# Normalised features of the next layer made inside three stages, and the scan's selection matrix made one stage earlier

## What is computed

```python
h = h + _L0_attn_ref(_layernorm(h, axis=-1), ...)   # state-space scan, 16 states
h = h + _L0_ffn_ref(_layernorm(h, axis=-1), ...)    # 15 experts, and a shared expert
h = h + _L1_attn_ref(_layernorm(h, axis=-1), ...)   # gated recurrence (GRU)
h = h + _L1_ffn_ref(_layernorm(h, axis=-1), ...)    # ternary weights, gelu, layernorm
h = h + _L2_attn_ref(_layernorm(h, axis=-1), ...)   # linear attention

def _layernorm(x, axis=-1, eps=1e-05):
    m = jnp.mean(x, axis=axis, keepdims=True)
    v = jnp.var(x, axis=axis, keepdims=True)
    return (x - m) / jnp.sqrt(v + eps)
```

## Time and profile before

| | us |
|---|---|
| median of 3 runs (1618.41 to 1622.33) | 1618.63 |
| the profiled execution | 1631.85 |
| its span | 1630.1 |
| busy PE, DVE, ACT, POOL | 1137.5, 1096.1, 676.5, 477.9 |
| granted TensorE clock, mean, as a share of full speed | 0.774 |

### The profile page before, as it was taken

The page is one execution under the profiler, slowest core; times in us unless marked ns, Lnnn a source line. Parts: engine busy times, 40 slices in busy tenths (PEclk is TensorE's granted clock), DMA queues, the critical chain, the costliest instruction groups (busy, mean ns, idle before and its releaser), DMA issues. The chain is left out here.

```text
span 1630.1 us, 31525 instructions
## 1 busy us (share of the span) xinstructions
PE 1137.5 (70%) x9868; PEld 814.8 (50%) x9868; DVE 1096.1 (67%) x2322; ACT 676.5 (42%) x1332; POOL 477.9 (29%) x614
## 2 busy tenths in 40 slices
PE   4514887774479998684857868365588886469992
PEld 2211232223368885352545745144476774469882
DVE  3864999994936554547867754888677766446553
ACT  4514655552045553214425722243365664224440
POOL 0042677762355554520001100000033332231203
PEclk9557899995589998787877977588566555569996
DMA  6500000001043334212000000000022221101113
GB/s 203 190 3 10 1 1 0 1 1 46 1 140 90 118 90 132 72 39 78 1 1 1 1 1 0 0 0 0 28 79 77 89 92 53 46 24 44 44 31 110
DMA packets 33968, 78.92 MB, mean 48 GB/s; under 512 B 6839, under 2 KB 22899, under 8 KB 30963
## 3 DMA queue, kind: packets, MB, share of 16 engines
q1 hardware_dynamic: 26800, 57.51, 10.3%
q0 software_dynamic: 6912, 18.88, 4.2%
q10 hardware_dynamic: 144, 1.05, 0.2%
HBM read 61.38 MB, written 16.04 MB: 47 GB/s over the span
## 5 line engine op out<-in xcount | busy, mean ns | idle before, releaser
L942 POOL TENSOR_TENSOR scan_ch<-scan_hs,scan_ct 128x452 f32<-128x452 f32 x128 | 143.3, 1140 | 58.8 <-DVE scan_hs L1054 52.4
L967 PE MATMUL scan_py<-scan_ch,ident 128*128 128x452 f32 x256 | 131.9, 606 | 40.4 <-POOL scan_ch L942 30.8
L1054 DVE TENSOR_TENSOR_SCAN scan_hs<-scan_abar,scan_bx 128x452 f32<-128x452 f32 x128 | 134.0, 1096 | 0.6 <-ACT scan_abar L1016 0.5
L2558 POOL TENSOR_TENSOR mha_prob_lo<-mha_prob,mha_prob_hi 113x452 f16<-113x452 f32 x64 | 65.4, 1043 | 137.7 <-ACT mha_prob_hi L2719 137.7
L457 PE MATMUL m0x_ph<-m0x_xb,m_w_hi 128*128 128x128 f16 x456 | 99.2, 220 | 0.2
L458 PE MATMUL m0x_ph<-m0x_xb,m_w_hi 128*128 128x128 f16 x456 | 99.1, 219 | 0.0
L459 PE MATMUL m0x_ph<-m0x_xb,m_w_lo 128*128 128x128 f16 x456 | 98.7, 218 | 0.0
L967 PEld LDWEIGHTS scan_py<-scan_ch,ident 128*128 128x128 f32 x256 | 41.4, 195 | 111.1 <-POOL scan_ch L942 99.9
L1641 DVE TENSOR_SCALAR m3x_a<-m3x_ph,m3x_b 128x128 f32<-128x128 f32 x184 | 49.7, 345 | 68.9 <-ACT m3x_ah L1602 67.0
L1016 ACT ACTIVATE scan_abar<-ssm_dt,ssm_a 128x448 f32<-128x448 f32 x128 | 80.6, 638 | 23.2 <-DVE scan_hs L1054 21.8
L1638 DVE SCALAR_TENSOR_TENSOR m0x_a<-m0x_ph,m0x_b,m0x_gate 128x128 f32<-128x128 f32 x114 | 34.7, 347 | 75.8 <-issue 38.2
(11 more groups left out here) (699 smaller groups left out, 4033.0 us busy)
## 6 DMA issues: line engine op xcount, KB each, us to landing
mha_wbuf<-m3w SPq DMA_DIRECT2D x16, 1024.0 KB, 4.6
tok_wbuf<-m0w SPq DMA_DIRECT2D x15, 768.0 KB
m_out<-m0x_yo SPq DMA_DIRECT2D x57, 128.0 KB
m_out<-m3x_yo SPq DMA_DIRECT2D x23, 128.0 KB
m_rows<-m0f_parts SPq DMA_DIRECT2D x4, 448.0 KB
m_rows<-m3f_parts SPq DMA_DIRECT2D x4, 448.0 KB
out<-h SPq DMA_DIRECT2D x4, 448.0 KB
tok_pt_f<-patches SPq DMA_DIRECT2D x1, 1728.0 KB, 8.1
```

What stands on the lines that cost most here:

```text
L942: pool.tensor_tensor(ch[r][:], hs[r][:], ct[n % 2][:], ALU.mult).then_inc(weighed, 1)
L967: pe.matmul(py[c][:, 0:GT], core.ident[:], ch[u % R][:], start=n == 0, stop=n == NS - 1).then_inc(summed, 1)
L1054: dve.tensor_tensor_scan(hs[u % R][:], abar[c][:, 0:GT], bx[u % R][:], 0.0, ALU.mult, ALU.add).then_inc(scanned, 1)
L2558: pool.tensor_tensor(prob_lo[g][:], prob[g % 2][:], prob_hi[g][:], ALU.subtract).then_inc(p_low, 1)
```

## The change

**Selection matrix.** `ssm.sel` lives beside the other inputs of the scan. POOL makes it in `stage_ssm_inputs`: a memset and two selects on 128 x 32 numbers, then one copy that spreads each over 128 columns. In the scan it is only read.

**Features of the next layer.** A new class `NextFeatures` does the work of the two stages group by group inside shared (for gru), gru (for bgm) and bgm (for la). The six stages between them go. DVE takes statistics and moments of a group (`stats`, `moments`), POOL raises the variance to -0.5 and multiplies (`scale`), ACT normalises (`normalise`, into one of two buffers), PE transposes one half of the features (`turn`), ACT and DVE write the high and the low half (`high`, `low`). PSUM banks for this are taken from the stages: shared has two px and pg in place of three and gives two banks, bgm one `po` in place of two and gives one, gru gives one that was free.

```diff
+class NextFeatures:
+    def stats(self, dve, b):
+        dve.bn_stats(self.six[:, b, :], self.core.h[:, b, :]).then_inc(self.counted, 1)
+    def moments(self, dve, q):
+        g = slice(q * GB, (q + 1) * GB)
...
+        dve.wait_ge(self.counted, (q + 1) * GB)
...
+        dve.tensor_scalar(var, var, 1.0 / D, EPS, ALU.mult, ALU.add).then_inc(self.var_ready, 1)
+    def scale(self, pool, q):
...
+        pool.wait_ge(self.var_ready, q + 1)
+        pool.tensor_tensor(self.rstd[:, g], self.var[:, g], self.half[:, g], ALU.pow).then_inc(self.raised, 1)
+        pool.wait_ge(self.raised, q + 1)
+        pool.tensor_tensor(self.shift[:, g], self.nmean[:, g], self.rstd[:, g], ALU.mult).then_inc(self.rstd_ready, 1)
+    def normalise(self, act, q):
+        act.wait_ge(self.rstd_ready, q + 1)
+        need(act, self.turned, (q - 1) * KC)
+        for j in range(GB):
+            b = q * GB + j
+            act.activation(self.xr[q % 2][:, j, :], self.core.h[:, b, :], ACT.Identity, bias=self.shift[:, b:b + 1],
+                           scale=self.rstd[:, b:b + 1]).then_inc(self.normed, 1)
+    def turn(self, pe, q, c):
+        n = q * KC + c
+        pe.wait_ge(self.normed, (q + 1) * GB)
+        need(pe, self.lo_done, n + 1 - self.banks)
...
+    def high(self, act, q, c):
+        act.wait_ge(self.turned, n + 1)
...
+    def low(self, dve, q, c):
+        dve.wait_ge(self.hi_done, n + 1)
...
 # stage_ssm_inputs, POOL
+                made.step(pool.memset(sel_rows[:], 0.0))
+                for part in range(2):
+                    made.step(pool.affine_select(out=sel_rows[:], in_=sel_rows[:], compare_op=ALU.not_equal, fill=1.0,
...
+                made.step(pool.tensor_copy(ssm.sel[:].rearrange("p a n m -> p (a n) m"),
+                                           sel_rows[:].unsqueeze(2).to_broadcast([128, 2 * NS, 128])))
 # stage_ssm_scan, POOL and PE
-                made.step(pool.memset(sel[:], 0.0))
-                for part in range(2):
-                    made.step(pool.affine_select(out=sel[:], in_=sel[:], compare_op=ALU.not_equal, fill=1.0,
...
-                pe.wait_ge(sel_made, 3)
 # stage_shared, POOL and PE
-                combine.gather(pool, core)
+                nx.begin(pool)
+                combine.gather(pool, core, range(3 * GB))
+                nx.scale(pool, 0)
+                combine.gather(pool, core, range(3 * GB, NB))
+                for q in range(1, NG):
+                    nx.scale(pool, q)
...
+                    if q >= 2:
+                        for c in range(KC):
+                            nx.turn(pe, q - 2, c)
                     outputs(q - 1)
-                outputs(NG - 1)
+                outputs(NG - 1, (0, 1))
+                for c in range(KC):
+                    nx.turn(pe, NG - 2, c)
+                outputs(NG - 1, (2, 3))
+                for c in range(KC):
+                    nx.turn(pe, NG - 1, c)
 # stage_gru, ACT
                     round_state(n - 1)
+                    q, e = unit(n)
+                    if q >= 2 and e == 0:
+                        nx.normalise(act, q - 2)
+                    if q >= 2 and e == 2:
+                        nx.high(act, q - 2, 0)
+                    if q >= 3 and e == 0:
+                        nx.high(act, q - 3, 1)
 # stage_bit_gelu, DVE (PE: turn in slots 2 and 3; ACT: normalise in slot 1, high in 2 and 3)
+                def following(q, j):
+                    if j == 0:
+                        dve.wait_ge(o_free, (q + 1) * GB)
+                        for i in range(GB):
+                            nx.stats(dve, q * GB + i)
+                        nx.moments(dve, q)
+                    if j >= 2:
+                        nx.low(dve, q, j - 2)
-                for q in range(NG + 2):
+                for q in range(NG + 3):
...
+                        if q >= 3:
+                            following(q - 3, j)
 # program
-            stage_norm_stats(nc, core, tag + "s", core.h)
-            stage_features(nc, core, tag + "f", core.h)
-            stage()
+        stage_gru(nc, core, d, gru, lambda st: PrepareLate(st, d, glu, mha))
+        stage_bit_gelu(nc, core, d, gelu)
+        stage_linear_attention(nc, core, d, linear)
```

More of the change, by code:

```diff
@@ L25 @@
 EPS = 1e-5
+NS = 16
 def wait_alone(eng, core, sem, value):
@@ L1696, in __init__, with gather @@
         self.added, self.picks_added = st.sem("added"), st.sem("picks_added")
-    def gather(self, pool, core):
+    def gather(self, pool, core, batches=range(NB)):
         m = self.m
-        for b in range(NB):
+        for b in batches:
             j = b % GB
@@ L1837, in _ @@
                         middle.on_scalar(act, n)
+                        if q >= 2 and f == 2:
+                            nx.normalise(act, q - 2)
                     high(q, FC - 1)
+                    if q >= 2:
+                        for c in range(KC):
+                            nx.high(act, q - 2, c)
+                for q in (NG - 2, NG - 1):
+                    nx.normalise(act, q)
+                    for c in range(KC):
+                        nx.high(act, q, c)
             @block.vector
@@ L1847, in low, with add @@
                     combine.add(dve, core, q, f)
-                def add(q):
-                    for j in range(GB):
+                def add(q, tiles=range(GB)):
+                    for j in tiles:
                         p, b = j % 2, q * GB + j
@@ L1871, in _ @@
                     low(q, FC - 1)
+                    if q >= 2:
+                        for c in range(KC):
+                            nx.low(dve, q - 2, c)
                     if q:
                         add(q - 1)
-                add(NG - 1)
+                        measure(q - 1)
+                for j in range(GB):
+                    add(NG - 1, (j,))
+                    if j == 1:
+                        for c in range(KC):
+                            nx.low(dve, NG - 2, c)
+                measure(NG - 1)
+                for c in range(KC):
+                    nx.low(dve, NG - 1, c)
 def stage_gru(nc, core, d, w, late):
@@ L1908, in _ @@
                     pool.memset(drive[p][:, :, 0:1], 0.5).then_inc(edges, 1)
+                nx.begin(pool)
                 late.on_pool(pool)
+                for q in range(NG):
+                    nx.scale(pool, q)
             @block.tensor
@@ L2003, in add, with measure @@
                                                  ALU.mult, ALU.add).then_inc(o_free[p2], 1)
+                def measure(q):
+                    for j in range(GB):
+                        dve.wait_ge(o_free[j % 2], q * 2 + j // 2 + 1)
+                        nx.stats(dve, q * GB + j)
+                    nx.moments(dve, q)
                 for n in range(N):
@@ L2011, in _ @@
                         add(q - 2, (2, 3))
+                        measure(q - 2)
                     dve.wait_ge(sig_ready, n + 1)
@@ L2017, in _ @@
                         split(n - 1)
+                    if q >= 2 and e == 2:
+                        nx.low(dve, q - 2, 0)
+                    if q >= 3 and e == 0:
+                        nx.low(dve, q - 3, 1)
                     late.on_vector(dve, n)
                 split(N - 1)
+                nx.low(dve, NG - 3, 1)
                 add(NG - 2, (2, 3))
-                add(NG - 1, (0, 1, 2, 3))
+                measure(NG - 2)
+                add(NG - 1, (0, 1))
+                for c in range(KC):
+                    nx.low(dve, NG - 2, c)
+                add(NG - 1, (2, 3))
+                measure(NG - 1)
+                for c in range(KC):
+                    nx.low(dve, NG - 1, c)
 def stage_bit_gelu(nc, core, d, w):
```

149 lines of the change are left out of this document (107 added, 42 removed).

## The result

The changed kernel takes 1622.72 us (median of 20 runs), the kernel before 1616.46 (median of 20 on the same chip): ratio 1.0032, 95% interval 1.0018 to 1.0047. The medians differ by 6.3 us and the ratio stands for 5.2: slower, just over what can be told from no change. The two profiled executions are not typical: 1631.85 before, 1611.37 after, so their spans must not be subtracted; the places have to be compared one by one.

The account below looks back on a forecast made before the run. DVE was taken to set the pace in gru and bgm. The terms -11.2 - 24.8 + 18.4 + 9.9 + 9.3 + 3.3 gave +4.9 us on the 1618.63 median: 1624 us, range 1608 to 1636.

Parts of the forecast that it names:

- Scan start: Selection matrix made earlier, in ssmin, so DVE's first scan product comes sooner: a gain of 11.2 us, bounds 9 and 12.
- Borders: Last add to next stage's first product: 9.65 us (shared), 11.05 (gru, bgm); 31.8 in place of 56.6, gaining 24.8.
- M: DVE's measuring of one group of four tiles, 4 statistics and 7 moment operations in chain: 2.5 us.
- P: POOL's power and product on 4 columns per group, with hand-overs: 2.0 us, the power taken as 1.6.
- rival B: No change: POOL's power on four columns costs as on one, 6.8 us less, 1617; chance 0.22.
- N: ACT's normalising of one group, 4 scaled activations of 256 columns at 0.49 us each: 1.65 us.
- Rival C: Much slower: POOL's power is paid per column, 16.6 us more, 1640; chance 0.12.
- Delay 1: Stage tails: PE waits before its last tiles until group 2 is normalised; 6.8 shared, 6.3 gru, 5.3 bgm, sum 18.4 us.
- Delay 2: Inside the stages: added work on DVE and ACT's queue lengthens gru by 9.9 us, bgm by 9.3, shared by 3.3.
- At no cost: Shared's last twelve POOL gathers now stand behind scale(0), hidden by an existing wait of 8.02 us; removed Sqrt loads save nothing.
- A: Faster: added work in gru units 6 to 11 and bgm groups 3 and 4 is hidden in waits, 1606; chance 0.20.
- D: The scan does not start sooner because something else was as late: 11.2 us more, 1635; chance 0.06.

Follow-up runs that it names:

- Moving the tiles forward: Changed kernel with group 2's transposes behind the last two output tiles in the tails of shared and gru: 1607.95 us, ratio 0.995 to the kernel before.
- second profile of the changed kernel: The changed kernel measured and profiled once more, unaltered: 1625.32 us, ratio 0.9992 to the kernel before.
- The second batch: Runs sharing one chip: the changed kernel again, all features at the tails, two variants of gru's part; the kernel before had median 1630.5 us there.
- the doubled statistics: Kernel with the selection matrix and bgm's features inside gru, its eight statistics inside the units done twice: 1626.69 us, ratio 0.9977 to the kernel before.
- the kernel with the matrix alone: Kernel before with only the selection matrix made in ssmin: 1618.08 us, ratio 0.9922.
- the one with shared's part: Kernel before plus the selection matrix in ssmin and gru's features inside shared: 1615.97 us, ratio 0.9905.
- gru's part alone: Kernel before plus the selection matrix in ssmin and bgm's features inside gru: 1624.22 us, ratio 0.9964.
- bgm's part alone: Kernel before plus the selection matrix in ssmin and la's features inside bgm: 1625.81 us, ratio 0.9963.
- the tails with the moments on DVE and on POOL: Matrix in ssmin, all features at stage ends; last batch against before: DVE moments 1580.23 us (0.9763); POOL moments for groups 0 to 2 1593.91 us (0.9851).

## Why the prediction was right, and where it was not

The forecast was +4.9 us and 1624, from a median of three runs; with 20 runs it is +5.2 by the ratio (+6.3 between the medians) and 1622.7. By its own steps:

**Scan start**, -11.2: measured -11.3 (-11.0 counted from the same instruction before ssmin). The Trainium skill's warning (GPSIMD Engine Reference, section 8) that POOL contends with DVE instructions that read two inputs in SBUF is borne out by the trace: 1.96 us for 0.69, and ssmin's first product 1.0 us later, which is what I had put on that case. The gain did not come down to 10 even so: in the changed kernel's profile DVE reaches the scan 0.75 us later, counted from the same instruction, in the others between 0.1 sooner and 1.0 later.

**Borders**, 9.65, 11.05 and 11.05: measured 9.3, 10.9 and 12.5 (bgm's last measure stood behind a low half that waited for ACT until 937.45, while its last add had ended at 936.90).

**Prices.** M 2.5 was 2.55. P 2.0 was 1.4 (707.61 to 709.01): the power on four columns takes 1.02 us against 0.86 on one, so rival B's price was nearly the right one (1.25). N 1.65 was 2.07, since the activation with scale and shift from a column takes 586 ns and not 492 as the one of the earlier trace rows. M, P and N together were 6.0 for 6.15: the two errors nearly cancel, which is one reason why B's 1617 did not come although its price nearly did. Rival C is out.

**Delay 1**, 6.8 and 6.3 and 5.3. From the last add of group 2 to the last add of group 3 the trace of before has 7.2 us in shared and in gru, that of the changed kernel 14.1 and 13.4: +6.9 and +6.2. In bgm it is 7.4 and 11.3, +4.0. Moving the tiles forward gave back 6.5 in shared and 5.0 in gru.

**Delay 2**, gru 9.9: measured 10.4, the same in four profiles. The two measures cost 4.9 for 5.0; DVE's waits for ACT 3.8 (1.72 + 2.04) for the 2.3 of two stalls; three low halves 1.6, and the fourth stands behind the last split; the 0.4 of PE's second transposition can't be told apart. So the DVE terms were right, and ACT's queue was undersized by 1.5. Bgm 9.3: from its first product to the last low half 93.4 and 93.9 against 85.7 to 87.3, some 7.3. The held ACT is seen at 917.13, behind POOL for 2.43 us, and DVE's wait for it at 920.47, 3.66 us. Shared 3.3 can't be measured alone, since its stretch scatters by 4 us without features.

**At no cost.** This held: in the second profile of the changed kernel the gather behind `scale(0)` still waited 3.69 us for an add of DVE, in place of 8.02.

**Slips in the sum**, each of 0.35 us at most: four low halves of 0.6 are 2.4 and not 2.2, 5.65 - 4.85 is 0.8 and not 0.9, and in the tail of bgm the first transposition is counted with 0.7 where its price is 1.05.

**By border.** Shared, +1.3 in all: 118.7 and 120.0 with the features against a mean of 118.6 in six profiles without, from 116.3 to 120.7: +0.8, within the scatter. Gru +8.4: +9.6 (10.4 inside, -0.8 in the tail). Bgm +6.4: +4.8.

**What the sum did not have**: la, 75.5 and 75.6 in the two profiles of the changed kernel and 80.0 before. With -11.3 + 0.8 + 9.6 + 4.8 = +3.9 this gives -0.5. The second batch agrees with that (0.9992), the first measurement (1.0032) lies some 6 us above it. There the runs fall into groups: of the changed kernel's 20 three are at 1611 to 1615 and the others at 1621 to 1628 (the profile of 1611.37 is the one with 107.4 in shared), of the 20 of before fifteen are at 1612 to 1619 and five at 1621 to 1622. Taken group against group, the medians differ by -1.4 and +2.3 us. So a good part of the +5.2 is that the upper group was commoner with the changed kernel, which no term of my sum says, and why it was is not settled. The mechanisms and most of their sizes are shown in the stretches; that the total came out within 0.3 us of the forecast is luck in good part.

**Rivals.** A fell by 10.4 where it allowed 4, and by the doubled statistics. D fell by the kernel with the matrix alone. C fell by the power's price.

## What to carry to other kernels

Work moved out of a stage of its own into another stage is only free where the engine that sets the pace there isn't the one it needs; where DVE is at 35.68 of 37.00 us, it is paid in full, and the same work put behind the last unit, where DVE waits for PE, turned +15 us for three borders into some -18 (5 in shared, 7 in gru, 6 to 7 in bgm). In a tail, first issue what the last tile waits for, and only then the preparation of the next stage. An engine that takes over work from a busy one (here POOL with eight short operations) has to be priced as a chain first: 3.3 us a group against DVE's 2.8. And two kernels are to be compared stage by stage where whole executions differ by some 10 us for other reasons, over a stretch that holds only what changed.

## What the runs showed of the hardware that was not expected

**A DVE instruction beside a POOL copy.** The two-input instruction of ssmin ended 0.54 or 0.55 us after POOL's copy in 13 of 13 profiles, whether it began 1.2 or 1.5 us before the copy's end, as shown under the scan start.

**Shared has two levels.** Where the stage took 113.8 to 120.7 us, the waits of DVE in it have a row like this (kernel before, then the one with shared's part; total, times, longest):

```profile
DVE shared_a L1866 <- remote: 7.4, 2, 6.0
```

```profile
DVE shared_a L1977 <- remote: 10.6, 1, 10.6
```

In the profiles with 100.6 to 107.4 it is missing. "Remote" means that the trace shows no releaser. It comes with and without the change and by batch (all of the first two, none of the last two), and went with the higher median of the kernel before, 1630.5 for 1616 to 1618. Its cause is open.

**La goes with the clock.** Its first 50 us had a granted clock of 0.73 to 0.76 in the profiles with 80.0 to 81.4 us, and of 0.86 to 0.90 in those with 75.5 to 76.9, in 14 of 14. The level doesn't follow from whether bgm carries features: it was high with (after) and without (gru's part alone), and low with (bgm's part alone) and without (before). But it isn't chance alone either: each of the three kernels that were profiled twice, in different batches, had the same level both times (75.5 and 75.6, 76.1 and 76.9, 81.4 and 81.4). What sets it is open; 4 us of every comparison in this case hang on it. The comparison of the tails with the moments on DVE and on POOL is one of them.
